# Attention kernel: reciprocals in PSUM, shared bank for rows and output, new order of the steps

## What is computed

```python
def _ada_ln(x, c, W_ss, b_ss):
    mu = jnp.mean(x, axis=-1, keepdims=True)
    var = jnp.mean((x - mu) ** 2, axis=-1, keepdims=True)
    h = (x - mu) / jnp.sqrt(var + EPS)
    ss = jax.nn.silu(c) @ W_ss + b_ss
    scale, bias = jnp.split(ss, 2, axis=-1)
    return (1.0 + scale)[:, None, :] * h + bias[:, None, :]
xq = _ada_ln(x_q, t_vec, Wss_q, bss_q)
xkv = _ada_ln(x_kv, t_vec, Wss_kv, bss_kv)
q = (xq @ Wq + bq).reshape(B, Lq, nh, dh)
kv = (xkv @ Wkv + bkv).reshape(B, Lkv, 2, nh, dh)
scores = jnp.einsum('bqhd,bkhd->bhqk', q, k) / jnp.sqrt(jnp.float32(dh))
attn = jax.nn.softmax(scores, axis=-1)
out = jnp.einsum('bhqk,bkhd->bqhd', attn, v).reshape(B, Lq, H)
return x_q + (out @ Wp + bp)
```

## Time and profile before

| | us |
|---|---|
| median of 3 runs | 1285.41 (1282.66 to 1286.21) |
| profiled execution | 1281.65, span 1279.8 |
| PE busy | 1189.2 (93%) |
| DVE busy | 1165.7 (91%) |
| POOL busy | 972.0 (76%) |
| ACT busy | 903.9 (71%) |
| mean granted TensorE clock | 0.979 of full speed |

### The profile page before, as it was taken

One profiled execution on the slowest core, in us unless ns is written; L12 is line 12 of the kernel. 1 busy time (PEld: TensorE's weight loads), 2 busy tenths in 40 slices (PEclk: granted clock), 3 DMA queues, 4 the chain that ended last, 5 costly groups with the idle time before them and its releaser, 6 DMA issues.

```text
span 1279.8 us, 33552 instructions
## 1 busy us (share of the span) xinstructions
PE 1189.2 (93%) x11072; PEld 697.8 (55%) x11072; DVE 1165.7 (91%) x1797; ACT 903.9 (71%) x1688; POOL 972.0 (76%) x1202
## 2 busy tenths in 40 slices
...
DMA packets 59865, 111.91 MB, mean 87 GB/s; under 512 B 6412, under 2 KB 6440, under 8 KB 59832
## 3 DMA queue, kind: packets, MB, share of 16 engines
...
## 4 chain that ended last, share of the span: by engine, by line
DVE 54%; issue 23%; PE 8%; ACT 3%; POOL 1%; DVEq 1%; ACTq 1%; POOLq 0%
DVE pr L879 14%; DVE pt_lo L907 10%; DVE pr L899 7%; DVE den L864 5%; DVE mx L887 5%; DVE xT_lo L849 4%; PE ps_q L1136 4%; DVE q_lo L917 3%; DVE oT_lo L856 3%; DVE rden L871 2%; PE ps_t L1170 2%; PE ps_s L1155 2%; DVEq L224 1%; ACT kb L526 1%; ACT xT_hi L509 1%
## 5 line engine op out<-in xcount | busy, mean ns | idle before, releaser
L879 DVE SCALAR_TENSOR_TENSOR pr<-pr,rden 128x512 f32<-128x512 f32 x256 | 295.7, 1194 | 4.4
L425 POOL TENSOR_TENSOR half_den<-pr 128x512 f32<-128x512 f32 x128 | 195.5, 1527 | 106.2 <-ACT pr L619 67.0
L568 ACT ACTIVATE q_hi<-ps_q,cur_bq 128x512 f16<-128x512 f32 x126 | 86.6, 687 | 197.5 <-PE ps_q L1136 173.2
L1170 PE MATMUL ps_t<-ident,pr 128*128 128x128 f32 x1024 | 164.0, 288 | 37.9 <-DVE pr L879 36.0
L418 POOL TENSOR_TENSOR xr<-y,xr 128x512 f32<-128x512 f32 x128 | 178.0, 1391 | 8.9 <-ACT y L534 8.9
L558 ACT CAST pt_hi<-ps_t 128x512 f16<-128x512 f32 x256 | 148.3, 588 | 46.5 <-PE ps_t L1170 41.7
L394 POOL TENSOR_TENSOR xr<-xr,bp_row 128x512 f32<-128x512 f32 x128 | 165.9, 1296 | 13.1 <-POOL rstd L373 6.9
L887 DVE TENSOR_REDUCE mx<-ps_s 128x8 f32<-128x512 f32 x256 | 163.2, 676 | 7.0 <-PE ps_s L1155 6.9
L907 DVE TENSOR_TENSOR pt_lo<-ps_t,pt_hi 128x512 f16<-128x512 f32 x256 | 163.0, 675 | 0.2 <-ACT pt_hi L558 0.2
L899 DVE TENSOR_TENSOR pr<-ps_s,mx 128x512 f32<-128x512 f32 x256 | 162.9, 675 | 0.0
L619 ACT ACTIVATE pr<-pr,exp_scale 128x1024 f32<-128x1024 f32 x128 | 146.2, 1142 | 12.6 <-DVE pr L899 12.2
...
## 6 DMA issues: line engine op xcount, KB each, us to landing
x_in<-in_x_dram SPq DMA_DIRECT2D x128, 256.0 KB, 2.6
xr<-in_x_dram SPq DMA_DIRECT2D x128, 256.0 KB, 2.8
out_dram<-xr ACTq DMA_DIRECT2D x128, 256.0 KB, 2.0
...
```

The costliest lines, as they stand in the source:

```text
L425: pool.tensor_tensor(half_den[:, :, :], pr[:, off % 2, :, 0:LKV // 2], pr[:, off % 2, :, LKV // 2:LKV], ALU.add).then_inc(half_done, 1)
L879: dve.scalar_tensor_tensor(out=pr[:, off % 2, hs, :], in0=pr[:, off % 2, hs, :], scalar=P_UNIT, in1=rden[:, hs].unsqueeze(2).to_broadcast( ...
L1170: last = pe.transpose(ps_t[:, h, P * g:P * (g + 1)], pr[:, off % 2, 2 * pair:2 * pair + 2, :].rearrange("p h l -> p (h l)"), ident[:, :])
```

## The change

- `rden` moves from SBUF to the second bank of ps_v. The turned rows of x go to the first bank, where the attention output already goes; `turn_x` and `weigh` each get a wait for the other's readers.
- DVE makes both `pt_lo` ahead of the maxima, and `xT_lo` after the subtractions. PE turns the weights one step later, right behind `score`; `turn_x` stands before `project_out`.
- The layernorm runs one unit further ahead (i+9). The row sum's activation gives the negative mean by its scale, so `neg_mean` on POOL goes; `veps` is one instruction instead of two.
- POOL makes `w_lo` and `w_tmp` right after the half sums, ahead of the row statistics, residual, `add_rows` and normalise.
- ACT's order: `y`, `oT_hi`, `pt_hi`, row sums, `xT_hi`, Exp, `q_hi`, squares, `w_hi`, then `values` (now step 1) or `key_blocks` (step 7). These two write whole blocks by a scale that is 1 or 0 per partition (masks from two sums over the identity), instead of parts of zeroed blocks.
- SP issues the stores, ahead of its loads.
- Steps of batch B - 2 are unrolled on all engines.

The diff without declarations, semaphore names and counts that follow from them:

```diff
@@ -55,6 +56,7 @@
         ps_v = psum("ps_v", [P, 2, 512])
 
         first_banks = (ps_q, ps_o)
+        rden = ps_v[:, 1, 0:NH]
 
 
         ident = sb("ident", [P, P], F32)
...
@@ -244,17 +243,18 @@
                 prime()
             for i in range(PER):
                 step(0, i)
-            with eng.Fori(1, B - 1) as b:
+            with eng.Fori(1, B - 2) as b:
                 for i in range(PER):
                     step(b, i)
-            for i in range(PER):
-                step(B - 1, i)
+            for b in (B - 2, B - 1):
+                for i in range(PER):
+                    step(b, i)
             for i in range(4):
                 step(B, i)
 
         def x_bank(b, off):
 
-            return ps_t[:, 0, :] if isinstance(b, int) and unit(b, off) < PER else ps_v[:, 1, :]
+            return ps_t[:, 0, :] if isinstance(b, int) and unit(b, off) < PER else ps_v[:, 0, :]
 
         def place(copy, part, t):
 
@@ -296,9 +296,16 @@
                 wait(sp, stored[off % 4], 16 * (2 * b + off // 4))
                 sp.dma_start(xr[:, off % 4, :], x_units[unit(b, off)]).then_inc(xr_loaded[off % 4], 16)
 
+            def store(b, off):
+                if not exists(b, off):
+                    return
+                wait(sp, y_ready, upto(b, off))
+                sp.dma_start(out_units[unit(b, off)], xr[:, off % 4, :]).then_inc(stored[off % 4], 16)
+
             def step(b, i):
+                store(b, i - 4)
                 load_x(b, i + 12)
-                load_xr(b, i)
+                load_xr(b, i - 1)
 
             for f in range(4):
                 load_x(0, f)
@@ -316,6 +323,10 @@
             for b in (B - 2, B - 1):
                 for i in range(PER):
                     step(b, i)
+            for i in range(4):
+                step(B, i)
+            for s in stored:
+                sp.wait_ge(s, 16 * (UNITS // 4))
 
 
         @block.gpsimd
@@ -325,18 +336,13 @@
             pool.affine_select(out=ident[:, :], in_=ident[:, :], compare_op=ALU.not_equal, fill=1.0,
                                base=0, pattern=[[-1, P]], channel_multiplier=1).then_inc(id_ready, 1)
             pool.memset(half_neg[:, :], -0.5).then_inc(consts_ready, 1)
-            pool.memset(eps[:, :], EPS).then_inc(consts_ready, 1)
-            pool.memset(over_h[:, 0:1], -1.0 / H).then_inc(consts_ready, 1)
-            pool.memset(over_h[:, 1:2], 1.0 / H).then_inc(consts_ready, 1)
             pool.memset(one_half[:, :], 0.5).then_inc(consts_ready, 1)
             pool.memset(ones[:, :], 1.0).then_inc(consts_ready, 1)
             pool.memset(lim[:, 0:MAX_SC + 3], 0.0).then_inc(consts_ready, 1)
             pool.memset(lim[:, MAX_SC + 3:MAX_SC + 4], H ** -0.5).then_inc(consts_ready, 1)
             pool.memset(lim[:, MAX_SC + 4:LIMS], 0.0).then_inc(consts_ready, 1)
-            pool.memset(kb[:, :, :, :, :], 0.0).then_inc(bd_ready, 1)
-            pool.memset(vb[:, :, :, :, :], 0.0).then_inc(bd_ready, 1)
-
-            pool.wait_ge(consts_ready, 9)
+
+            pool.wait_ge(consts_ready, 6)
             for half in range(2):
                 ts = slice(CT // 2 * half, CT // 2 * (half + 1))
                 pool.wait_ge(c_mv, CT // 2 * (half + 1))
@@ -351,25 +357,19 @@
                 pool.tensor_tensor(cT_lo[half][:, m, :], turned[n % TURNED], cT_hi[half][:, m, :].bitcast(F32),
                                    ALU.subtract).then_inc(cT_done, 1)
 
-            def mean(b, off):
+            def await_rows(b, off):
 
                 if exists(b, off):
-                    s = off % 2
-                    wait(pool, xh_ready, unit(b, off - 1))
-                    wait(pool, row_stats, 2 * unit(b, off) + 1)
-                    pool.tensor_tensor(neg_mean[:, s:s + 1], row_sum[:, s:s + 1], over_h[:, 0:1], ALU.mult)\
-                        .then_inc(mean_ready, 1)
+                    wait(pool, row_stats, 2 * upto(b, off))
 
             def moments(b, off):
 
                 if not exists(b, off):
                     return
                 s = off % 2
-                wait(pool, row_stats, 2 * upto(b, off))
-                pool.tensor_tensor(var[:, s:s + 1], row_sq[:, s:s + 1], over_h[:, 1:2], ALU.mult).then_inc(ln_step, 1)
-                wait(pool, ln_step, 3 * unit(b, off) + 1)
-                pool.tensor_tensor(veps[:, s:s + 1], var[:, s:s + 1], eps[:, :], ALU.add).then_inc(ln_step, 1)
-                wait(pool, ln_step, 3 * unit(b, off) + 2)
+                pool.tensor_scalar(veps[:, s:s + 1], row_sq[:, s:s + 1], 1.0 / H, EPS, ALU.mult, ALU.add)\
+                    .then_inc(ln_step, 1)
+                wait(pool, ln_step, 2 * unit(b, off) + 1)
                 pool.tensor_tensor(rstd[:, s:s + 1], veps[:, s:s + 1], half_neg[:, 0:1], ALU.pow)\
                     .then_inc(ln_step, 1)
 
@@ -377,7 +377,7 @@
 
                 if exists(b, off):
                     wait(pool, xT_turned, unit(b, off - 1))
-                    wait(pool, ln_step, 3 * upto(b, off))
+                    wait(pool, ln_step, 2 * upto(b, off))
 
             def normalise(b, off):
                 if exists(b, off):
@@ -446,20 +446,20 @@
 
             def step(b, i):
                 half_sums(b, i - 1)
-                mean(b, i + 8)
-                add_rows(b, i - 4)
-                moments(b, i + 8)
-                await_moments(b, i + 8)
-                residual(b, i - 3)
-                normalise(b, i + 8)
                 if 2 <= i <= 5:
                     scaled_wq_lo(b + 1, i - 2)
                 if 1 <= i <= 4:
                     scaled_wq(b + 1, i - 1)
+                await_rows(b, i + 9)
+                residual(b, i - 2)
+                moments(b, i + 9)
+                await_moments(b, i + 9)
+                add_rows(b, i - 4)
+                normalise(b, i + 9)
 
             def prime():
                 def layernorm(f):
-                    mean(0, f)
+                    await_rows(0, f)
                     moments(0, f)
                     await_moments(0, f)
                     normalise(0, f)
@@ -480,6 +480,7 @@
                 layernorm(6)
                 layernorm(7)
                 key_lo(CT - 1)
+                layernorm(8)
 
             every_step(pool, step, prime)
 
...
@@ -521,9 +522,9 @@
                 if not batch_exists(b):
                     return
                 wait(act, s_mm, PER * b)
-                for r in range(HPG):
-                    rows = slice(DH * r, DH * (r + 1))
-                    act.copy(kb[rows, :, :, r % 2, :], k16[rows, b, :, :, :]).then_inc(kb_done, 1)
+                for r in range(2):
+                    act.activation(kb[:, :, :, r, :], k16[:, b, :, :, :], ACT.Copy, scale=k_mask[:, r:r + 1])\
+                       .then_inc(kb_done, 1)
 
             def output(b, off):
                 if exists(b, off):
@@ -537,10 +538,9 @@
                 if not batch_exists(b):
                     return
                 wait(act, pv_mm, PER * b)
-                for part in range(2):
-                    for par in range(2):
-                        rows = slice(LKV * par, LKV * (par + 1))
-                        act.copy(vb[rows, part, :, par, :], v_all[rows, part, b, :, :]).then_inc(vb_done, 1)
+                for par in range(2):
+                    act.activation(vb[:, :, :, par, :], v_all[:, :, b, :, :], ACT.Copy, scale=v_mask[:, par:par + 1])\
+                       .then_inc(vb_done, 1)
 
             def query_bias(b):
                 if not batch_exists(b):
@@ -572,15 +572,13 @@
                 if exists(b, off):
                     wait(act, x_loaded[off % 4], 16 * (2 * b + off // 4 + 1))
                     wait(act, row_stats, 2 * unit(b, off))
-                    wait(act, mean_ready, unit(b, off - 1))
-                    act.activation(junk[:, :], x_in[:, off % 4, :], ACT.Copy,
-                                   accum_out=row_sum[:, off % 2:off % 2 + 1]).then_inc(row_stats, 1)
+                    wait(act, xh_ready, unit(b, off - 1))
+                    act.activation(junk[:, :], x_in[:, off % 4, :], ACT.Copy, scale=-1.0 / H,
+                                   accum_out=neg_mean[:, off % 2:off % 2 + 1]).then_inc(row_stats, 1)
 
             def sum_squares(b, off):
 
                 if exists(b, off):
-                    wait(act, mean_ready, upto(b, off))
-                    wait(act, ln_step, 3 * unit(b, off - 1))
                     wait(act, row_stats, 2 * unit(b, off) + 1)
                     act.activation(junk[:, :], x_in[:, off % 4, :], ACT.Square, bias=neg_mean[:, off % 2:off % 2 + 1],
                                    accum_out=row_sq[:, off % 2:off % 2 + 1]).then_inc(row_stats, 1)
@@ -593,34 +591,29 @@
                 act.copy(w_hi[:, :, m * P:(m + 1) * P], w_tmp[:, :, :]).then_inc(w_hi_done, 1)
 
             def step(b, i):
-                sum_rows(b, i + 8)
                 output(b, i - 4)
-                if not (isinstance(b, int) and b == 0 and i == 0):
```

(55 more changed lines are left out.)

25 lines of the change are left out of this document (12 added, 13 removed).

## The result

| us | before | after |
|---|---|---|
| median of 4 runs each | 1284.04 (1281.76 to 1286.21) | 1385.86 (1382.74 to 1389.37) |
| profiled execution, span | 1279.8 | 1387.5 |
| mean granted TensorE clock | 0.979 | 0.956 |

The kernel after takes 1.0794 times as long, 95% interval 1.076 to 1.0828: 7.9% slower. The forecast was 1360, range 1325 to 1400, slower: the time lies in the range, 26 above the forecast.

What follows compares the result with a forecast made beforehand. Before, VectorE bound at 8.63 us a step, TensorE next at 8.31; after, the GpSimd-ScalarE-TensorE loop in w steps. 1281.65 + 90.6 - 17.4 + 1.5 = 1356, on the runs' median 1360 us; range 1325 to 1400.

Steps and rivals of the forecast that it cites:

- batch 0: First batch: 1.5 us more, because the two halves of Wp lie on ScalarE and VectorE in the same chain.
- the last batch: Batch without layernorm or w operations: 79.3 us instead of 96.7, 17 less, with line 879's pair no longer stretched.
- the prologue: Work before the loop, with unit 8's layernorm added and waits for `neg_mean` gone: 0, within 2 us both ways.
- the ring: Loop through ScalarE's `w_hi`, GpSimd's `w_lo` to normalise, and TensorE's next `turn_x`: 4.10 + 6.46 = 10.56 us with both w operations.
- the four long steps: Steps 2 to 5 of a batch, with w operations on GpSimd: 11.66, 10.56, 10.86 and 9.56 us against 8.31.
- the plain steps: Steps without w operations: loop 3.60 + 4.22 = 7.8 us, shorter than TensorE's 8.31, so it costs nothing.
- B: Rival: the loop doesn't bind, TensorE sets the pace; batches of 69.1 us, 1242 on the median, faster; chance 0.09.
- C: Rival: line 879's pair stays stretched with `rden` in PSUM; 46 us more, 1406; chance 0.05.
- D: Rival: transfers of `xr` land late in plain steps; 30 us more, 1390; chance 0.10.
- E: Rival: loop partly hidden, about 1 us shorter per w step; 60 us less, 1300; chance 0.06.
- the late Exp: ScalarE's Exp in step 2, delayed by `values` in step 1: 1.1 us late, making that step 11.66.

Runs made afterwards that it cites:

- whi_early: Kernel after, with ScalarE's `w_hi` moved ahead of the row sums and GpSimd's order kept: 1264.31 us, 0.9852 times before.
- rows_first: Kernel after, with GpSimd's `add_rows` and residual ahead of `w_lo` and two small additions in their place: 1272.99 us, 0.992 times before.

## Why the prediction was right, and by how much it was off

**The sum,** for the profiled executions. From the first maxima of batch 0 to those of the last batch it is 1310.74 - 120.44 = 1190.3 us, before 1185.50 - 122.61 = 1062.9: 127.4 more where 90.6 + 1.5 were forecast. The last batch with its tail takes 76.8 instead of 94.3, 17.5 less (forecast 17.4); the prologue 2.2 less (forecast 0, within 2). 127.4 - 17.5 - 2.2 = 107.7, and 33 of it is what the forecast lacked (26 between the medians).

**Right: the ring.** Its path, the four long steps and their size stood in the forecast as the traces show them: 4.10 + 6.46 = 10.56 against 4.26 + 6.62 = 10.88. The signs named for it came: TensorE idle before `turn_x` 115.2 us (forecast 140), GpSimd idle before `w_lo` 3.6 each (forecast 3), VectorE busy 106 us less (forecast 120), steps as in the table. whi_early and rows_first take the ring away from either side and with it 121.5 and 113 us, so it is shown and not only argued.

**Mis-sized: each long step, by 0.1 to 0.6.** In step 3 ScalarE's `xT_hi` began 0.76 after `turn_x` instead of 0.64 (0.69 in steps 4 and 5); GpSimd's residual to `veps` took 1.35 instead of 1.25 and `rstd` to the next 0.68 instead of 0.63. In step 2 Exp came later than the 1.1 forecast; ScalarE in the kernel after:

```profile
621.49 1.15 ACT L604 ACTIVATE pr<-pr,exp_scale 128x1024 f32<-128x1024 f32 x1 [1.41 <-DVE pr L896]
```

That is 2.64 behind its `turn_x`, against 632.36 - 631.11 = 1.25 in step 3: 1.4 late. `values` began 4.17 behind its `turn_x` instead of 4.0, and VectorE has `oT_lo` (0.60) to do ahead of the two `pt_lo`, which the forecast's chain to Exp left out. Small terms, but a ring adds up every one of them: the batch shown is 1.8 above the forecast, the 14 behind batch 0 on average (1190.3 - 84.9)/14 = 78.96, 2.1 above. 14 x 2.1 = 30 of the 33. Part of it is the clock, which the forecast left out. In a later batch the lower clock meets `turn_x` itself; TensorE in the kernel after:

```profile
867.27 1.12 PE L1116 MATMUL ps_v<-ident,xh 128*128 128x128 f32 x4 [3.38 <-POOL xh L385]
```

ScalarE's `xT_hi` begins at 868.42, 1.15 behind it, and the step takes 11.26.

**Mis-sized: the plain steps, slightly.** Forecast was that a plain step's loop is 7.8 and so hidden below TensorE's 8.31. Steps 1 and 6 took 8.26, but step 0 took 8.63 with `turn_x` waiting 0.26 for `xh`. GpSimd in that step of the kernel after:

```profile
684.65 1.27 POOL L394 TENSOR_TENSOR xr<-xr,bp_row 128x512 f32<-128x512 f32 x1 [4.12 <-ACT junk L583]
...
687.11 1.27 POOL L418 TENSOR_TENSOR xr<-y,xr 128x512 f32<-128x512 f32 x1 [0.28 <-POOL rstd L373]
```

From `turn_x` at 680.55 the residual starts 4.10 later instead of 3.60 (0.21 of it a wait of Exp, after the late step 7), and the rest takes 689.18 - 684.65 = 4.53 instead of 4.22. A slack of 0.5 was thinner than it looked.

**Missed: batch 0.** It took 84.9 us, forecast 78.3. The stretch from 125 to 150 us in the kernel after (length, busy time and instructions of PE, PEld, DVE, ACT, POOL, granted clock, DMA share, GB/s), and then in the kernel before:

```profile
125.00:150.00 25.00, 13.51 (x88) 7.30 (x84) 13.91 (x21) 12.50 (x22) 8.76 (x10) 0.66 0.16 53
```

```profile
125.00:150.00 25.00, 18.28 (x153) 10.67 (x152) 19.86 (x30) 18.30 (x36) 15.06 (x25) 0.76 0.22 65
```

Its first two steps take 11.8 and 12.3 (`turn_x` at 124.26, 136.03 and 148.33); with the two halves of Wp in them 8.3 and something was forecast. The trace shows both the halves of Wp and the clock. In each step VectorE waits for ScalarE's `wp_hi` (2.67 and 1.78 us), so TensorE waits 5.24 and 5.18 for VectorE; the matmuls behind that take 136.03 - 130.94 = 5.09 and 148.33 - 142.88 = 5.45, where the loop has 2.59 and 3.52: 4.4 us more, at a granted clock of 0.50 in the first. No run separates the two; together they are 6.6 us of 1387.

**The last batch** went as forecast: GpSimd's stretch is gone from the pair, and steps of 6.66 follow each other at its end. VectorE in the kernel after, the answer to the earlier trace rows:

```profile
1349.79 1.28 DVE L884 TENSOR_REDUCE mx<-ps_s 128x8 f32<-128x512 f32 x2
...
1356.45 1.28 DVE L884 TENSOR_REDUCE mx<-ps_s 128x8 f32<-128x512 f32 x2
```

**The rivals.** B (TensorE sets the pace, 1242) fell for this kernel. whi_early, which has no late `w_hi`, came to 1264, so B's own sum was 22 too low: with the ring cut, `turn_x` still waits 20.8 us and `score` 32.1. C (the pair stays stretched) fell with 680/683/691. D (late `xr` loads) fell: of the 163.5 us that the residual waits, 148.8 end with ScalarE's squares and only 14.7, in six executions, with a load, and a load lands in 2.9 us. E (a ring 1 us shorter) fell: the ring was 0.3 longer, not shorter. The 18 us allowed for the sizes of the long steps would not have covered the 26; with the 15 for the late Exp and the prologue the range held. All of the error lay on one side.
